# Two transformer blocks on one core: order lists for four engines behind layer 0's self-attention, silu in pairs, MLP products in halves

## The chip, the core and the metric

One core of a Trainium2 chip. The metric is the device time of one execution in microseconds, the median of several runs. Times inside a run come from one profiled execution; they count from the first instruction of its span.

## What is computed

Two blocks in a row on x of 2 batches x 512 tokens x 128 channels, 16 heads of 8 channels.

```python
# layer 0, per batch (c: 128 values, context: 77 x 128, its own layer norm)
x = x + gate_a * (softmax(q k^T / sqrt(8)) v @ W_proj + b_proj)       # 512 x 512 per head, of modulate(ln(x))
x = x + softmax(qc kc^T / sqrt(8)) vc @ W_cproj + b_cproj             # 512 x 77 per head, q of ln(x)
x = x + gate_m * (gelu(modulate(ln(x)) @ W_mlp1 + b) @ W_mlp2 + b)    # 512 hidden
# layer 1, per batch (tokens rolled by 32)
x = x + g_msa * (softmax in windows of 64 tokens @ w_so + b_so)
x = x + g_mca * (softmax over the 16 largest of 77 scores, v, @ w_co + b_co)
x = x + g_mlp * ((silu(a) * b) @ w_m2 + b_m2), a, b = two halves of ln(x) mod @ w_m1    # 2 x 512 hidden
```

## The kernel before

All tensors stay in SBUF; each engine (PE, DVE = VectorE, ACT = ScalarE, POOL, and SP for transfers) runs its own list of instructions in order, and semaphores hold an instruction until its inputs are there. PSUM is cut into six rooms (X0, X1, M0, M1 of one bank, W0, W1 of two); `rooms_in_turns` gives each product its room and its turn in it, `open_room` (L242) makes PE wait until the last user of the room has been read, `read_room` makes the reader wait until it is filled.

Layer 0's self-attention is one loop over 32 heads with a look-ahead (`STEPS`): PE multiplies scores for the maxima (L1504), DVE reduces them (L1221), PE multiplies again with the negated maximum folded in (L1527), ACT takes the exponential (L814), PE multiplies with V (L1542). It ends near 154.6 us.

Behind it stands code in fixed loops, on which this case bears:
- Layer 0's cross-attention, 16 halves (8 heads of 128 tokens each; batch 0 is halves 0 to 7): PE scores (`cross_scores`, L1574), DVE maximum and subtraction (L1275, L1280), ACT exponential (L896), PE turn of the weights (`cross_turn`, L1585), ACT copies (L930), per two halves PE product with V (`cross_pv`, L1597), ACT copy (L832), PE turn (L1557), DVE divide (L1051, L1054). `e` counts the halves; the steps of the next and the last half are written into one turn of the loop on each engine.
- Around it, per batch: turn of the heads (`o_turn`, L1390), projection (`project`, L1401), residual (L1063), layer norm statistics (L973 to L980), its power on POOL (L618), normalization (L985), turn (`ln_T`, L1348), shift and scale on ACT (L767), the next projection.
- The MLP: four chunks of 128 hidden (`mlp_in`, L1673; layer 1 also L1677), gelu (L953) or silu (L958) with the gate product on DVE (`gate_mul`, L1195), and one product `mlp_out` (L1413) over all four chunks that starts when the last chunk is there.
- Layer 1's window attention: per batch eight q and k products (`window_qk`, L1368), their copies on DVE and ACT (L1000, L805), V (L1375, L1009), 8 maxima products with reductions (`window_maxima`, L1612, L1174), the maxima turned, negated (L1178) and sent by SP into rows of Q (L519). Batch 0 is done with its maxima before batch 1 begins, and both before the first window. Then eight windows S (scores, L1641), exponential (L823), V (L1654), turn (L1555), divide (L1185, L1187) in the order of the string `WINDOWS`.
- Layer 1's cross-attention with top-k, 16 halves: PE scores, ACT copy (L902), DVE per half 8 times max (L1294), replace (L1297), max (L1301), replace (L1304); POOL takes the first maximum off (L732), ACT the exponentials of difference (L915) and of what was replaced (`left`, L920), POOL multiplies both (L736), PE turns, and so on as in layer 0. All of the MLP comes behind the last half.

```python
ARRIVE = ({"oT": -1, "out": 1, "lnT": 3, "qc": 5}, {"oT": 2, "out": 3, "lnT": 4, "qc": 5})
WINDOWS = "S0 S1 V0 S2 V1 T0 S3 V2 T1 S4 V3 T2 S5 V4 T3 oT S6 V5 T4 out S7 T5 lnT qc".split()
for e in range(-1, HALVES + 3):        # PE
    if e + 1 < HALVES:
        cross_scores(layer, e + 1)
    if 1 <= e <= HALVES:
        cross_turn(layer, e - 1)
    if e % 2 == 0 and 1 <= e // 2 <= B * NT:
        cross_pv(layer, e // 2 - 1)
```

Of the kernel before, what the change touches and what calls it, by code (L numbers as in the profile page):

```python
# [51 lines left out]
WINDOWS = "S0 S1 V0 S2 V1 T0 S3 V2 T1 S4 V3 T2 S5 V4 T3 oT S6 V5 T4 out S7 T5 lnT qc".split()  # L52
WINDOWS_LATE = {0: ("V6",), 1: ("V7", "T6"), 2: ("T7",)}
# [10 lines left out]
ARRIVE = ({"oT": -1, "out": 1, "lnT": 3, "qc": 5}, {"oT": 2, "out": 3, "lnT": 4, "qc": 5})  # L64
# [28 lines left out]
GATE_SPAN = ((0, 2), (2, 5))  # L93

# [10 lines left out]
def rooms_in_turns():  # L105
# [21 lines left out]
    for layer in range(2):  # L127
        if layer == 1:
            for b in range(B):
                if b:  # L130
                    use("M", "lnT", 3, 1)
                for c in range(NQ):
                    use("M", "qkv", 1, b, "q", c)
                    use("X", "qkv", 1, b, "k", c)
                use("M", "qkv", 1, b, "v")
                for i in range(NT):
                    for half in range(2):
                        use("W", "maxw", b, i, half)
                use("M1", "mT", 1, b)
        if layer == 0:  # L140
            for t in range(STEPS):
                j = t - LOOK - 1
                for q in range(NT):
                    if t < HEADS:
                        use("Y", "max", t, q)
                    for half in first_halves(t - LOOK, q):
                        use("W", "sT", 0, t - LOOK, half)
                    if q == 1 and t % G == 0 and 1 <= t // G <= B * NG:
                        use("Y", "mT", 0, t // G - 1)
                    if q == 2 and j % NT == 0 and 0 <= j < UNITS:  # L150
# [1651 lines left out]
```

## Time and profile before

| | us |
|---|---|
| median of 3 runs | 452.52 (448.51 to 453.73) |
| the profiled execution | 449.5 |
| its span, first to last instruction | 447.7 |

| engine | busy us | share |
|---|---|---|
| PE, products | 362.2 | 81% |
| PE, weight loads (beside products) | 205.6 | 46% |
| DVE | 297.6 | 66% |
| ACT | 203.8 | 46% |
| POOL | 112.0 | 25% |

The engines work side by side, so shares don't add up; what counts in a stretch is which engine's wait ends last. The granted clock is 1.00 when TensorE runs at 2.4 GHz and 0.5 when it runs at 1.2 GHz; between them is a mean over the stretch.

### The profile page before, as it was taken

What the parts mean: (1) busy time and instruction counts of PE and PEld (TensorE: products, weight loads), DVE (VectorE), ACT (ScalarE), POOL (GpSimd) and SP (SyncE); (2) the same over time, 40 slices, a digit from 0 to 9 for tenths busy, and PEclk for the clock granted to TensorE, in tenths of its full rate; (3) what the DMA queues carried; (4) which work ended last, traced back from release to release, by engine and by line L of the source; (5) the groups of instructions that cost most, each with busy time, mean ns of one, the idle gap of its engine ahead of it and who ended that gap; (6) DMA issues with size and microseconds to landing.
All of it is one profiled execution on the core that took longest, in us unless ns stands there. A gap on an engine that the chain in (4) does not pass through costs nothing.

```text
span 447.7 us, 8982 instructions
## 1 busy us (share of the span) xinstructions
PE 362.2 (81%) x3317; PEld 205.6 (46%) x3317; DVE 297.6 (66%) x1279; ACT 203.8 (46%) x303; POOL 112.0 (25%) x130
## 2 busy tenths in 40 slices
PE   2988999999999879898798889956576566674885
PEld 2334223323332357676555467733354334454454
DVE  4677668899893175665437371247989999996342
ACT  2320345666758645667331124413445355654411
POOL 5362110490010120002206000022442544443020
PEclk9995589999999999999999685868876878886999
DMA  7247350410000000000000000000000000000000
GB/s 205 39 152 215 107 159 3 124 46 1 2 1 3 0 1 2 1 2 0 1 1 2 4 3 6 4 1 1 1 1 1 1 2 1 1 1 1 1 24 25
DMA packets 13247, 12.88 MB, mean 29 GB/s; under 512 B 2373, under 2 KB 11681, under 8 KB 13203
## 3 DMA queue, kind: packets, MB, share of 16 engines
q1 hardware_dynamic: 13007, 12.28, 10.1%
q8 instruction: 27, 0.44, 0.4%
q14 instruction: 17, 0.14, 0.1%
q0 software_dynamic: 160, 0.01, 0.0%
q10 hardware_dynamic: 36, 0.01, 0.0%
HBM read 9.41 MB, written 2.63 MB: 27 GB/s over the span
## 4 chain that ended last, share of the span: by engine, by line
PE 53%; DVE 29%; ACT 7%; issue 5%; DMA 3%; POOL 1%; SPq 1%; ACTq 0%; DVEq 0%; POOLq 0%
PE psum L1504 5%; PE psum L1574 5%; PE psum L1542 5%; DVE left L1297 4%; DVE left L1304 4%; PE psum L1527 4%; PE psum L1368 3%; DVE mx L1221 3%; PE psum L1673 3%; DVE top L1294 3%; DVE top L1301 3%; PE psum L1557 3%; PE psum L1585 2%; DVE xhat L985 2%; PE psum L1597 2%
## 5 line engine op out<-in xcount | busy, mean ns | idle before, releaser
L1221 DVE TENSOR_REDUCE mx<-psum 128x1 f32<-128x512 f32 x128 | 81.3, 682 | 17.2 <-PE psum L1504 13.8
L814 ACT ACTIVATE big<-psum 128x1024 f32<-128x1024 f32 x64 | 62.1, 1022 | 42.5 <-PE psum L1527 26.9
L618 POOL TENSOR_TENSOR rstd<-vareps,minus_half 128x4 f32<-128x4 f32 x12 | 12.2, 1020 | 160.0 <-DVE vareps L980 159.8
L1574 PE MATMUL psum<-kblk,qf 128*128 128x308 f32 x128 | 47.2, 501 | 1.1 <-DVE qf L1168 0.8
L1504 PE MATMUL psum<-KS,QS 72*128 72x512 bf16 x112 | 43.8, 420 | 4.9 <-DVE mx L1221 3.7
L1585 PE MATMUL psum<-ident,pr 128*77 128x128 f32 x256 | 38.4, 299 | 10.3 <-POOL pr L736 10.3
L1585 PEld LDWEIGHTS psum<-ident,pr 128*77 128x77 f32 x256 | 34.5, 167 | 18.5 <-POOL pr L736 13.8
L736 POOL TENSOR_TENSOR pr<-pr,early 128x616 f32<-128x616 f32 x16 | 23.9, 1493 | 55.9 <-ACT early L920 34.9
L1542 PE MATMUL psum<-big,V 128*9 128x512 f32 x256 | 34.8, 616 | 0.5 <-ACT big L814 0.5
L1597 PE MATMUL psum<-QS,vc 77*9 77x128 f32 x256 | 13.8, 342 | 24.2 <-ACT QS L930 24.1
L1527 PE MATMUL psum<-QS,KS 75*128 75x512 bf16 x112 | 32.8, 379 | 0.4
L1574 PEld LDWEIGHTS psum<-kblk,qf 128*128 128x128 f32 x128 | 26.9, 231 | 11.5 <-issue 4.9
L1504 PEld LDWEIGHTS psum<-KS,QS 72*128 72x128 bf16 x112 | 10.4, 102 | 46.0 <-issue 21.4
L1051 DVE RECIPROCAL rden<-psum 128x16 f32<-128x16 f32 x24 | 6.0, 250 | 34.8 <-PE psum L1557 34.8
L1297 DVE MATCH_REPLACE8 left<-top,gates 128x77 f32<-128x77 f32 x128 | 26.9, 224 | 0.0
L1304 DVE MATCH_REPLACE8 left<-top,left 128x77 f32<-128x77 f32 x128 | 26.9, 225 | 0.0
L1063 DVE TENSOR_TENSOR x<-psum,x 128x512 f32<-128x512 f32 x12 | 8.3, 690 | 24.6 <-PE psum L1401 14.5
L767 ACT ACTIVATE hT<-psum,mod 128x512 f32<-128x512 f32 x10 | 7.8, 776 | 36.4 <-PE psum L1348 36.4
L930 ACT ACTIVATE big<-psum 77x512 f32<-77x512 f32 x32 | 17.1, 586 | 12.6 <-PE psum L1585 12.5
L1294 DVE MAX8 top<-gates 128x8 f32<-128x77 f32 x128 | 19.4, 225 | 3.8 <-ACT gates L902 3.8
L732 POOL TENSOR_TENSOR early<-gates,top 128x616 f32<-128x616 f32 x16 | 19.6, 1223 | 8.6 <-DVE top L1294 8.2
L902 ACT ACTIVATE gates<-psum 128x616 f32<-128x616 f32 x16 | 10.9, 681 | 22.3 <-PE psum L1574 22.2
(202 smaller groups left out, 666.1 us busy)
## 6 DMA issues: line engine op xcount, KB each, us to landing
QS<-scr_q SPq DMA_DIRECT2D x7, 288.0 KB
KS<-scr_k SPq DMA_DIRECT2D x7, 288.0 KB
scr_q<-qp SPq DMA_DIRECT2D x2, 384.0 KB, 3.1
scr_k<-kp SPq DMA_DIRECT2D x2, 384.0 KB, 3.8
gates<-scr_g SPq DMA_DIRECT2D x2, 320.0 KB, 4.3
early<-in_L_xcond_w_ada_dram SPq DMA_DIRECT2D x1, 576.0 KB, 5.3
scr_k<-kp SPq DMA_DIRECT2D x2, 256.0 KB, 4.3
wmlp<-in_L_xcond_W_mlp_dram SPq DMA_DIRECT2D x2, 256.0 KB, 3.2
```

The source lines that it names most:

```text
L736: pool.tensor_tensor(pr[:, k, :], pr[:, k, :], taken[:, k, :], ALU.mult).then_inc(s_pr, 1)
L814: freed(act.activation(pT[:, u % 2, 1024 * half:1024 * (half + 1)], ps, ACT.Exp), "sT", 0, u, half)
L1221: freed(dve.tensor_reduce(mx[:, n % 3, at:at + 1], ps, AX_X, ALU.max), "max", t, q)
L1294: dve.max(top[:, k, h, 0:8], row(sc, h)).then_inc(s_top, 1)
L1297: dve.match_replace(out=row(left, h), in_to_replace=top[:, k, h, 0:8], in_values=row(sc, h), imm_value=-BIG).then_inc(s_top, 1)
L1304: ins_ = dve.match_replace(out=row(left, h), in_to_replace=top[:, k, h, 8:16], in_values=row(left, h), imm_value=-BIG)
L1504: filled(pe.matmul(ps, QS[b][0:ROWS, h, q * P:(q + 1) * P], KS[b][0:ROWS, h, :], start=True, stop=True), "max", j, q)
L1527: last = pe.matmul(ps[:, t * N:(t + 1) * N], KS[b][0:ROWS + 3, h, kt * P:(kt + 1) * P], QS[b][0:ROWS + 3, h, :], start=True, stop=True)
L1542: last = pe.matmul(ps[QUAD * hh:QUAD * hh + DV, :], V[:, b, kt, G * g + hh, :], pT[:, j % 2, hh * N:(hh + 1) * N], start=(kt == 0), stop=( ...
L1574: last = pe.matmul(ps[:, 512 * a:512 * a + HH // 2 * S], qf[:, b, i * P:(i + 1) * P], kb[:, c0:c0 + HH // 2 * S], start=True, stop=True)
L1585: last = pe.transpose(ps[0:S, t * P:(t + 1) * P], pr[:, e % 2, S * h:S * (h + 1)], ident[:, :])
L1597: last = pe.matmul(ps[q:q + DV, c * P:(c + 1) * P], vc[:, layer, b, h, :], pcT[layer][:, s % 2, h, :], start=True, stop=True)
```

## The change

Everything from the end of layer 0's self-attention on is no longer loops but five tables: `PE_ORDER`, `DVE_ORDER`, `ACT_ORDER` and `POOL_ORDER` list the pieces of each engine one by one, and `RINGS` gives the PSUM rooms of each kind of piece. A piece is `kind.layer or batch.number`: `sc` scores, `T` turn of weights, `C` product with V, `D` its turn and divide, `oT`, `out`, `lnT`, `qc` the steps around it, `mlp0`/`mlp1` the first MLP products, `mo` the halves of `mlp_out`, `wqk`/`wv`/`max`/`mT` the window projections and maxima, `S`/`V`/`W` the window's scores, product and turn with divide, `first8`/`next8` the two parts of a half's top-k, `res`/`stat`/`norm`/`rstd`/`bias` the residual and layer norm.

```diff
+PE_ORDER = pieces("""
+    T.1.9 sc.1.13 oT.3.0 out.4.0 C.1.4 T.1.10 T.1.11 sc.1.14 lnT.5.0 sc.1.15 C.1.5 mlp1.0.0 T.1.12 T.1.13
...
+ACT_ORDER = pieces("""
+    oT.0.1 ex.0 ex.1 T.0.0 T.0.1 ex.2 ex.3 T.0.2 C.0.0 T.0.3 ex.4 lnT.1.1 ex.5 T.0.4 ex.6 T.0.5 ex.7 T.0.6
...
+    copy.14 left.12 mlp.1.0.0 mlp.1.0.1 diff.13 T.1.12 left.13 diff.14 copy.15 C.1.5 T.1.13 left.14
+    mlp.1.0.2 mlp.1.0.3 diff.15 left.15 C.1.6 T.1.14 T.1.15 C.1.7 oT.3.1 lnT.5.1 mlp.1.1.0 mlp.1.1.1
...
+POOL_ORDER = pieces("""
+    bias.2.1 blocks.1.1 rstd.3.1 bias.3.0 rstd.4.0 diff.0 diff.1 mult.0 bias.3.1 mult.1 diff.2 diff.3
+    rstd.4.1 diff.4 mult.2 mult.3 mult.4 diff.5 mult.5 diff.6 mult.6 diff.7 diff.8 mult.7 diff.9 mult.8
...
+RINGS = {('sc', 0): ('W0', 'W1'), ('sc', 1): ('W0', 'W1'), ('T',): ('X1',), ('C',): ('W0',), ('D',): ('X0',),
...
-        pcT = [big[0:S, :, :].rearrange("p k (h t) -> p k h t", h=H),
-               QS[0][0:S, :, :].rearrange("p h t -> p (h t)").bitcast(F32).rearrange("p (k h t) -> p k h t", k=2, h=H)]
+        pW = [[wqr[:, :], kp[:, :, :, :].rearrange("p b j t -> p (b j t)").bitcast(F32)[:, 2 * N:3 * N]],
+              [old[:, B * NT * H * 2 * DV:B * NT * H * 2 * DV + N], wkv[:, :]]]
+        pcT = QS[0][0:S, :, :].rearrange("p h t -> p (h t)").bitcast(F32).rearrange("p (k h t) -> p k h t", k=2, h=H)
...
-            def mlp_out(n, b):
+            def mlp_out(n, b, part):
...
+                for c in (2 * part, 2 * part + 1):
+                    for i in range(NT):
                         last = pe.matmul(ps[:, i * C:(i + 1) * C], gT[:, b, c, i * P:(i + 1) * P],
-                                         gw[n, b][:, c * C:(c + 1) * C], start=(c == 0), stop=(c == NC_ - 1))
-                filled(last, "out", n, b)
+                                         gw[n, b][:, c * C:(c + 1) * C], start=(c == 0 and i == 0), stop=(c == NC_ - 1 and i == NT - 1))
+                if part:
+                    filled(last, "out", n, b)
...
+            def gated_mlp_in(b, pair):
+                for c in (2 * pair, 2 * pair + 1):
+                    ps = open_room(pe, "mlp", 1, b, c)
...
+                ps = open_room(pe, "mlpb", b, pair)
+                for j in range(2):
...
+            for piece in PE_ORDER:
+                kind, args = piece[0], piece[1:]
+                if kind == "sc":
+                    cross_scores(*args)
```

So that pieces may cross, some buffers move: the window exponentials (`pW`) and layer 0's turned weights (`pcT`) leave `big`, in which the gelu and gate outputs lie, and the spread window weights (`wqkF`) leave `left` for `V`; POOL therefore spreads them behind the last product with V of layer 0's self-attention (`spread` in its list). Layer 1's second MLP halves come in pairs of chunks into one room of two banks (`mlpb`).

The new order on two engines. First DVE around layer 1's window maxima, before: L1000 copies q, L985 normalizes batch 1, L1009 adds the bias to V, L1174 reduces maxima, L1178 negates them.

```order
L973 BN_STATS stats<-x 128x6 x4
L977 BN_AGGR mv<-stats 128x2 x4
L980 TENSOR_SCALAR vareps<-mv 128x4
L1000 TENSOR_SCALAR KS<-psum,colsF 128x512 x4
L985 TENSOR_SCALAR xhat<-x,mv,rstd 128x128 x4
L1009 TENSOR_TENSOR QS<-psum,wide 64x64x8 x2
L1174 TENSOR_REDUCE mxw<-psum 128x8 x8
L1178 TENSOR_SCALAR mneg<-psum 64x128
```

The same place now, where the lines are L1057 (q), L1043 (normalization), L1066 (V), L1229 (maxima) and L1235 (negation):

```order
L1057 TENSOR_SCALAR KS<-psum,colsF 128x512
L1229 TENSOR_REDUCE mxw<-psum 128x8 x2
L1057 TENSOR_SCALAR KS<-psum,colsF 128x512
L1229 TENSOR_REDUCE mxw<-psum 128x8
L1066 TENSOR_TENSOR QS<-psum,wide 64x64x8 x2
L1057 TENSOR_SCALAR KS<-psum,colsF 128x512
L1229 TENSOR_REDUCE mxw<-psum 128x8 x2
L1057 TENSOR_SCALAR KS<-psum,colsF 128x512
L1229 TENSOR_REDUCE mxw<-psum 128x8
L1057 TENSOR_SCALAR KS<-psum,colsF 128x512
L1229 TENSOR_REDUCE mxw<-psum 128x8 x3
L1235 TENSOR_SCALAR mneg<-psum 64x128
```

Batch 1's q copies stand between batch 0's reductions, and the negation of batch 0 behind the first reduction of batch 1; before, batch 0's eight reductions and its negation came ahead of all of batch 1. Second, PE at the end of layer 1's top-k, before: L1585 turns weights, L1597 multiplies with V, L1557 turns for the divide, L1673 and L1677 are the first MLP products, L1390 turns the heads, L1401 projects, L1413 is the second MLP product.

```order
L1585 MATMUL psum<-ident,pr 77x128 x8
L1597 MATMUL psum<-QS,vc 9x128 x16
L1557 MATMUL psum<-ident,qp 128x128 x4
L1673 MATMUL psum<-hT,wm 128x512
L1677 MATMUL psum<-hT,wm 128x512
L1673 MATMUL psum<-hT,wm 128x512
L1677 MATMUL psum<-hT,wm 128x512
L1557 MATMUL psum<-ident,qp 128x128 x4
```

And now, with L1627 for the turn of weights, L1639 for the product with V, L1599 for the turn, L1705 and L1709 for the first MLP products, L1428 and L1439 for heads and projection, L1454 for a half of the second MLP product:

```order
L1705 MATMUL psum<-hT,wm 128x512 x2
L1709 MATMUL psum<-hT,wm 128x512 x2
L1454 MATMUL psum<-wm,big 128x128 x8
L1627 MATMUL psum<-ident,pr 77x128 x8
L1599 MATMUL psum<-ident,qp 128x128 x4
L1454 MATMUL psum<-wm,big 128x128 x8
L1627 MATMUL psum<-ident,pr 77x128 x8
L1639 MATMUL psum<-QS,vc 9x128 x16
L1599 MATMUL psum<-ident,qp 128x128 x8
L1428 MATMUL psum<-ident,res 128x128 x4
L1439 MATMUL psum<-gw,res 128x128 x4
```

Batch 0's MLP products all stand ahead of the last turns of batch 1, and nothing stands between these turns, the heads' turn and the projection; before, batch 0's MLP products stood between them.

## Rows read from the trace of the kernel before

**Rows 1.** The page's first line.

```profile
span 447.7 us, 8982 instructions
```

**Rows 2.** Stretches: us, busy PE, PEld, DVE, ACT, POOL, clock, DMA, GB/s.

```profile
154.60:208.40 53.80, 48.48 (x468) 36.04 (x467) 35.78 (x75) 30.57 (x56) 4.68 (x5) 0.97 0.01 2
208.40:232.60 24.20, 20.63 (x152) 14.77 (x151) 7.46 (x32) 11.15 (x17) 4.25 (x4) 1.00 0.00 1
232.60:269.30 36.70, 31.05 (x568) 20.05 (x566) 22.47 (x43) 7.56 (x10) 7.95 (x5) 0.80 0.01 3
269.30:304.90 35.60, 29.72 (x757) 22.63 (x757) 8.67 (x28) 12.97 (x25) 2.28 (x2) 0.64 0.02 4
304.90:407.50 102.60, 64.96 (x533) 44.77 (x531) 99.22 (x807) 50.59 (x85) 44.72 (x34) 0.80 0.00 1
407.50:447.70 40.20, 29.42 (x164) 19.26 (x164) 14.23 (x35) 12.97 (x19) 5.04 (x4) 0.92 0.05 14
```

**Rows 3.** Timeline, layer 0's cross-attention: start us, us, engine line op [idle before <-releaser].

```profile
165.79 1.10 PE L1597 MATMUL psum<-big,vc 77*9 77x128 f32 x16 [2.60 <-ACT big L930]
...
166.82 2.42 PE L1574 MATMUL psum<-kblk,qf 128*128 128x308 f32 x4
...
170.40 1.20 PE L1574 MATMUL psum<-kblk,qf 128*128 128x308 f32 x4
```

**Rows 4.** Timeline, the end of layer 0.

```profile
228.94 3.81 PE L1413 MATMUL psum<-gw,big 128*128 128x128 f32 x32 [0.43 <-ACT big L953]
```

**Rows 5.** Timeline, layer 1's projections and maxima; last row: transfers, us to landing.

```profile
240.54 1.39 DVE L1009 TENSOR_TENSOR QS<-psum,wide 64x512 f32<-64x512 f32 x2
...
247.37 1.29 DVE L1174 TENSOR_REDUCE mxw<-psum 128x8 f32<-128x512 f32 x2 [0.66 <-PE psum L1612]
...
250.92 8.88 PE L1368 MATMUL psum<-hT,left 128*128 128x512 f32 x16 [0.87 <-ACT hT L767]
...
L519 SPq DMA_DIRECT2D KS<-mneg x8: 502/589/592, 249.5 to 271.5; - x8
...
KS<-mneg SPq DMA_DIRECT2D x8, 8.0 KB, 1.9
```

**Rows 6.** Timeline, from the windows to the first top-k.

```profile
286.32 0.42 DVE L1187 TENSOR_TENSOR QS<-psum,rdenw 64x256 f32<-64x256 f32 x1
...
292.21 0.69 DVE L1063 TENSOR_TENSOR x<-psum,x 128x512 f32<-128x512 f32 x1 [5.47 <-PE psum L1401]
...
304.93 1.22 DVE L1294 MAX8 top<-gates 128x8 f32<-128x77 f32 x8 [3.23 <-ACT gates L902]
```

**Rows 7.** Top-k: timeline rows; VectorE's waits (us, times, longest).

```profile
310.50 1.22 DVE L1294 MAX8 top<-gates 128x8 f32<-128x77 f32 x8
...
338.52 1.10 DVE L985 TENSOR_SCALAR xhat<-x,mv,rstd 128x128 f32<-128x128 f32 x4
...
407.99 2.35 DVE L985 TENSOR_SCALAR xhat<-x,mv,rstd 128x128 f32<-128x128 f32 x4
...
DVE top L1294 <- ACT gates L902: 3.8, 3, 3.2
DVE x L1063 <- PE psum L1401: 2.1, 1, 2.1
```

**Rows 8.** Timeline, behind the last match.

```profile
415.14 0.60 ACT L832 ACTIVATE qp<-psum 128x512 f32<-128x512 f32 x1 [1.23 <-PE psum L1597]
...
415.75 1.28 ACT L958 ACT_TABLE_LOAD   x1
...
418.92 0.60 PE L1557 MATMUL psum<-ident,qp 128*128 128x128 f32 x4
...
423.53 0.60 PE L1390 MATMUL psum<-ident,res 128*128 128x128 f32 x4
...
432.18 1.10 PE L1673 MATMUL psum<-hT,wm 128*128 128x512 f32 x2 [0.92 <-issue]
...
444.07 0.69 DVE L1063 TENSOR_TENSOR x<-psum,x 128x512 f32<-128x512 f32 x1 [3.99 <-PE psum L1413]
```

More of the change, by code:

```diff
@@ new lines, in rooms_in_turns @@
+    for t in range(STEPS):
+        j = t - LOOK - 1
+        for q in range(NT):
+            if t < HEADS:
+                use("Y", "max", t, q)
+            for half in first_halves(t - LOOK, q):
+                use("W", "sT", 0, t - LOOK, half)
+            if q == 1 and t % G == 0 and 1 <= t // G <= B * NG:
+                use("Y", "mT", 0, t // G - 1)
+            if q == 2 and j % NT == 0 and 0 <= j < UNITS:
+                use("M0", "pv", 0, j // NT)
+        for item in EARLY.get(t, ()):
+            for kind, key in EARLY_ROOMS[item]:
+                use(kind, *key)
+        if j > 0 and j % NT == 0:
+            use("Y", "pvT", 0, j // NT - 1)
+        for at, key in ((T_OUT, ("oT", 0, 0)), (T_OUT + 2, ("out", 0, 0)),
+                        (T_OUT + 5, ("lnT", 1, 0)), (T_OUT + 7, ("qc", 0, 0))):
+            if t == at:
+                use("Y", *key)
@@ new lines, in turned_weights_out @@
+            def turned_weights_out(layer, f):
+                s = f // 2
+                if s >= 2 and f % 2 == 0:
+                    wait_full(act, "pvc", layer, s - 2)
+                for part in range(2):
+                    ps = read_room(act, "pT", layer, f, part)
+                    h0 = HH * (f % 2) + 4 * part
+                    freed(act.activation(pcT[:, s % 2, h0:h0 + 4, :], ps[0:S, :].rearrange("p (h t) -> p h t", t=P),
+                                         ACT.Copy), "pT", layer, f, part)
@@ new lines, in window_maxima @@
+                ps = row_groups(open_room(pe, "maxw", b, i, half))
+                for c in range(NQ):
+                    for j in range(2):
+                        for w in range(2):
+                            t0, q0 = i * P + w * WIN, QUAD * (2 * half + j)
+                            last = pe.matmul(ps[w * WIN:(w + 1) * WIN, j, c * WIN:(c + 1) * WIN],
+                                             QF[q0:q0 + QUAD, b, c, t0:t0 + WIN], KF[q0:q0 + QUAD, b, c, t0:t0 + WIN],
+                                             start=True, stop=True)
@@ new lines, in window_pv @@
+            def window_pv(u):
+                b, i = steps[u]
+                ps = open_room(pe, "pv", 1, u)
+                if i == 0:
+                    wait_read(pe, "qkv", 1, b, "v")
+                for half in range(2):
+                    wait_read(pe, "sT", 1, u, half)
+                for h in range(H):
+                    c, j = divmod(h, NQ)
+                    p0 = HALF * (j % 2) + WIN * c
+                    last = pe.matmul(ps[QUAD * j:QUAD * j + 2 * DV, c * WIN:(c + 1) * WIN],
+                                     VW[:, b, i, h, :, :].rearrange("p w e -> p (w e)"),
+                                     pW[u % 2][j // 2][:, p0:p0 + WIN], start=True, stop=True)
+                filled(last, "pv", 1, u)
```

1039 lines of the change are left out of this document (471 added, 568 removed), and 23 rows, old and new, of the table RINGS.

## The prediction

> **What bounds the kernel now.** I read the page first: the span is 447.7 us [rows 1], the execution it belongs to took 449.5, and the median of the three runs shown is 452.52, 3.0 above the profiled one. Then I cut the span into seven stretches at the places where the chain of waits changes its engine, and read the busy times of each [rows 2]. The first 154.6 us, layer 0's self-attention, keep their code and their order. After that no engine is full for long. From 154.6 to 208.4 (layer 0's cross-attention) TensorE is busy 48.5 of 53.8 us at a granted clock of 0.97: it is the bound, and only its stalls can go. From 208.4 to 232.6 (the end of layer 0) everything is one chain of small steps. From 232.6 to 269.3 (layer 1's projections and window maxima) TensorE is busy 31.1 and VectorE 22.5 of 36.7, taking turns at a granted 0.80. From 269.3 to 304.9 (windows) VectorE works 8.7 us of 35.6. From 304.9 to 407.5 (top-k) VectorE is busy 99.2 of 102.6: that is its floor. From 407.5 to the end, 40.2 us, it is a chain again. So a new order can win in the second, third, fourth and last of the stretches behind 154.6, and next to nothing in the top-k.
>
> **The change, stretch by stretch.** No matrix product, reduction or exponential is added or dropped; four table loads are added on ScalarE. What follows walks the new lists with the old durations.
>
> *Layer 0's cross-attention.* Now the output product of the heads' weights waits 2.60 us for ScalarE, because the third exponential stands ahead of the copies it needs, and VectorE does a residual and statistics before the third subtraction [rows 3]. Behind that idle time the score products run at half speed, 2.42 us for four where they take 1.20 later [rows 3]: 1.2 more. The new lists put sub.2 ahead of res.0.1, and the copies T.0.0 and T.0.1 ahead of ex.2, so I take both away (3.8) and give 0.5 back for new short waits: the eighth half's scores start about 3.3 earlier than now. From there TensorE has the same work as before.
>
> *The end of layer 0.* Now the out projection of batch 1 stands behind four MLP products, and the last MLP product of 3.81 us starts whole at 228.94 [rows 4]. In the new list one MLP product stands ahead of the last turn and one behind it, so res.1.1 is ready some 5.6 earlier; but lnT.2.1 stands behind mo.2.0.1, and that waits for the fourth gelu, which gives most of it back. The half products let the last MLP product end some 0.9 earlier than it would. Both together: layer 1 starts at 228.4 instead of 232.6, a gain of 4.2.
>
> *Projections and maxima.* Now two batches of projections and two batches of maxima stand one behind the other, 36.7 us. In the new list the windows' scores S.0 may start once the first batch's negated maxima lie in their rows. Of VectorE's 22.5 us in this stretch [rows 2] the list puts one V copy of 1.39, seven of sixteen reductions (two take 1.29, so 4.5) and a negation of about 0.3 behind that point [rows 5], 6.2 in all: 16.3 stay ahead of it. Walking the list I find 5.0 of waits (the first projections, the first maxima, batch 1's transposed activations). Four row transfers of about 0.6 us each to issue and 1.9 to land follow [rows 5], 4.3. Sum 25.6: a gain of 11.1. TensorE's share fits into it: its 31.1 us shrink with the clock, since the second batch's projections, 8.88 of them, ran partly at the lower one [rows 5].
>
> *Windows.* From S.0 to the first eight maxima 35.6 now, of which 17 to the last divide of batch 0 at 286.3, 6 to its residual at 292.2 and 12.7 to the first maximum at 304.93 [rows 6]. The new list has four windows, not six, ahead of that divide, but two maxima products and S.4 ahead of oT.2.0, and S.4 must wait for the second batch's rows, again 4.3 behind a negation. I get 14.8, then 7.4 and 12.7: 34.9, a gain of 0.7.
>
> *Top-k.* A half of 8 heads takes 5.57 us (310.50 less 304.93), sixteen take 89.1 [rows 6, 7]. VectorE's waits inside the stretch are 0.6 for ScalarE's copies (3.8 less the 3.2 ahead of the first) and 2.1 for batch 1's out projection [rows 7]; other VectorE work is then 102.6 - 89.1 - 2.7 = 10.8. The new list moves a normalization (1.1) and two gate products (taken at a residual's 0.69 each) in and two divides (an estimate of 0.5 each) out: +1.5 [rows 6, 7]. Two normalizations now stand beside a POOL product each. Now one such takes 2.35 us where another takes 1.10 [rows 7], so I add 2.5. Walking ScalarE's list with its silu pairs I find each score copy ready 1.5 us or more before VectorE asks, so no wait is added, and the old 2.7 go: 89.1 + 10.8 + 1.5 + 2.5 = 103.9, a loss of 1.3. That cover is thin: a silu pair costs ScalarE two loads of 1.28 and two silus, about 4 us, where it has some 2 us idle per half, twice.
>
> The Trainium skill, ScalarE: Activation LUTs, section What ACT_TABLE_LOAD costs, says that each switch costs the load of 1283 ns and a drain of some 1380 ns, and that calls should be batched by table set, against what this change does. The trace agrees with the load and shows no drain: the copy before it ends at 415.74 and the load begins at 415.75 [rows 8]. By the row four more loads are 5.1 us of ScalarE, by the rule 10.6, of which two would lie on the last chain, 2.8 more than I count.
>
> *The tail.* Now, behind the last match at 407.5, the last turn stands behind four MLP products (418.92), and the turn for the out projection behind four more (423.53); the second batch's MLP starts at 432.18 and the last residual at 444.07 [rows 8]. In the new list the gates gate.0.2 and gate.0.3 follow the last match, mo.5.0.1 holds T.1.15 back until +5.0, and the turn oT.3.1 comes at +9.2 instead of +16.0: 6.8 gained. From there to the MLP is as before. Its two half products let the first half run ahead of the last two gates: 10.7 instead of 11.9 to the last residual. The exp load ahead of the last left.15 costs 0.5, counted in the +9.2. Sum: a gain of 8.0.
>
> Sum: 4.2 + 11.1 + 0.7 - 1.3 + 8.0 = 22.7. On the profiled 449.5 that is 426.8. The median of the runs shown is 3.0 above that execution; I add about half of this and forecast 428.
>
> **Bounds.** The walk is optimistic, since every list is in order and a late input stops all that stands behind it. Unshown is TensorE's clock under the new order. It is granted 0.80 in the maxima and 0.64 in the windows now [rows 2]; I took mixed clock for the first and the low one for the second. As estimates from the 29.7 and 31.1 us of TensorE there [rows 2]: at full clock in the windows too a quarter of the 29.7 goes, 8 us (420); at the low one in the maxima too 0.3 of the 31.1 come back, 9 us (437).
>
> **Rivals.**
> *A cold TensorE in layer 1* (437). For it: maxima of 64 columns with waits between them are where the clock falls now [rows 2]. Against: they stand among dense projections now.
> *Top-k waits* (436). POOL's list puts diff.3, rstd.4.1 and diff.4 ahead of mult.2, so turned weights come late; if half of the sixteen halves wait 1 us each, +8. For it: VectorE's floor has no room. Against: the only score copy that hangs on mult.2 is some 3 us early.
> *The stalls only move* (449.5): in-order lists stop at pieces that come late, as S.4 ahead of oT.2.0 does, and eat the gain. For it: four engines' lists cross in hundreds of places. Against: the tail's 6.8 and the maxima's overlap rest on few steps.
> *Slower: layer 0's cross-attention at half clock* (455 and up). It is the one long stretch where TensorE is the bound, at 0.97 [rows 2], and there half speed costs its whole time: four score products take 2.42 instead of 1.20 [rows 3]. If finer order leaves more pauses and it runs low, 48.5 us of busy time become up to 97; above about half of the stretch the 24 us gained are gone. Against: the lists take waits out there. The Trainium skill, TensorE: Matmul & The Clock Gate, section HAM oscillation, says that pauses between bursts throw the array back to half clock again and again; the drop at 166.8 behind an idle wait agrees.
>
> **How the numbers follow.** Forecast (420 to 433) 0.50, cold TensorE 0.18, top-k waits 0.17, stalls moved 0.09, slower 0.06. The range of 418 to 443 holds the first three. About 1% (448 to 457) is what a measurement tells from no change: faster is 0.85, the same 0.09, slower 0.06.
>
> **What would show it.** Right: layer 1's first projection near 228, the first window scores near 254, the first top-k maximum near 289, the last match near 392, 32 us behind it. Wrong: a top-k of more than 106 us (the second rival), windows later than 260 (the first), granted clock under 0.9 in layer 0's cross-attention (the last), or a tail still above 37 us.

## The result and the profile after

The changed kernel takes 435.53 us (median of 4 runs, 431.75 to 440.47) where the kernel before takes 452.97 beside it: a ratio of 0.9606, 95% interval 0.9539 to 0.9674. Forecast were 428 and 418 to 443. In a second comparison it took 434.34, ratio 0.9644 (0.9593 to 0.9695). Ratios, here and below, are of the runs within 1.5% of the fastest of their kernel, medians of all runs. The profiled execution took 431.75, 17.7 us below that of before; the sum had promised 22.7 on the same base.

The page's first line of the changed kernel:

```profile
span 430.0 us, 9048 instructions
```

Its stretches, cut where those of [rows 2] were cut (first cross scores, last turn of layer 0's weights, first projection of layer 1, first window scores, first top-k maximum, last match, end); columns as there:

```profile
152.80:201.40 48.60, 45.97 (x469) 35.99 (x466) 38.43 (x75) 31.12 (x56) 9.17 (x10) 1.00 0.01 2
201.40:227.70 26.30, 20.79 (x149) 14.32 (x150) 12.22 (x32) 11.41 (x17) 7.55 (x5) 1.00 0.00 1
227.70:256.20 28.50, 27.21 (x487) 16.70 (x489) 19.18 (x38) 7.45 (x10) 2.26 (x2) 0.96 0.02 4
256.20:291.50 35.30, 29.40 (x845) 23.31 (x839) 11.96 (x34) 13.11 (x25) 1.02 (x1) 0.69 0.02 4
291.50:395.20 103.70, 71.19 (x545) 48.23 (x546) 103.32 (x812) 57.88 (x93) 48.38 (x37) 0.80 0.00 1
395.20:430.00 34.80, 23.90 (x155) 16.59 (x154) 10.78 (x31) 10.14 (x16) 3.79 (x3) 0.85 0.06 16
```

Measured from the first row of one operation to the first row of the next (the last match: to its end), in the profiles of both kernels:

| stretch | before | after | moved | predicted |
|---|---|---|---|---|
| start to first cross scores | 154.7 | 152.9 | -1.9 | 0 |
| to layer 1's first projection | 77.9 | 74.8 | -3.0 | -4.2 |
| to the first window scores | 36.7 | 28.6 | -8.2 | -11.1 |
| to the first top-k maximum | 35.6 | 35.3 | -0.4 | -0.7 |
| to the last match | 102.6 | 103.7 | +1.1 | +1.3 |
| to the end | 40.1 | 34.8 | -5.3 | -8.0 |

The first line is no gain of the change. In thirteen profiles of kernels whose lists agree up to there, the first cross scores come between 151.4 and 158.8 us. So what follows compares stretches, not the clock time of an event. Three stretches gave less than promised: 1.2, 2.9 and 2.7 us.

What is new at the end of layer 0, in the timeline of VectorE (DVE), POOL and TensorE (PE):

```profile
195.03 4.07 DVE L1043 TENSOR_SCALAR xhat<-x,mv,rstd 128x128 f32<-128x128 f32 x4
212.20 2.88 DVE L1043 TENSOR_SCALAR xhat<-x,mv,rstd 128x128 f32<-128x128 f32 x4 [1.13 <-POOL rstd L686]
219.46 4.02 DVE L1043 TENSOR_SCALAR xhat<-x,mv,rstd 128x128 f32<-128x128 f32 x4 [1.12 <-POOL rstd L686]
...
195.27 1.28 POOL L749 TENSOR_TENSOR x<-x,gb 128x512 f32<-128x512 f32 x1
196.50 2.26 POOL L757 TENSOR_TENSOR kblk<-kcT,mask 128x1232 f32<-128x1232 f32 x1
212.12 2.10 POOL L706 COPY QS<-blank 128x2304 f32<-128x2304 f32 x1
219.39 1.27 POOL L749 TENSOR_TENSOR x<-x,gb 128x512 f32<-128x512 f32 x1
220.62 2.27 POOL L757 TENSOR_TENSOR kblk<-kcT,mask 128x1232 f32<-128x1232 f32 x1
...
201.44 1.10 PE L1627 MATMUL psum<-ident,pr 128*77 128x128 f32 x8 [1.57 <-ACT pr L943]
```

The same kernel's view of the normalization's line from 194.9 to 224 us (shortest, median and longest instruction in ns; first and last start):

```profile
L1043 DVE TENSOR_SCALAR xhat<-x,mv,rstd x12: 334/352/2305, 195.0 to 223.1; 128x128 f32<-128x128 f32 x12
```

Four instructions of some 0.34 us each make a normalization; undisturbed it takes 1.1, as in [rows 7]. Here three take 4.07, 2.88 and 4.02 us, and one single instruction 2305 ns, which is as long as the POOL instruction beside it (2.26, 2.27). Behind the first of them TensorE waits 1.57 us for the last exponential.

The windows, the top-k's table load and the tail, in the timeline of the same kernel:

```profile
274.99 1.64 PE L1667 MATMUL psum<-KS 32*64 32x64 f32 x64 [1.25 <-DMA KS<-mneg]
...
377.92 0.80 ACT L966 ACTIVATE early<-left,negbig 128x616 f32<-128x616 f32 x1
378.73 1.28 ACT L990 ACT_TABLE_LOAD   x1
...
404.18 0.63 PE L1428 MATMUL psum<-ident,res 128*128 128x128 f32 x4 [0.77 <-DVE res L1111]
413.31 3.75 PE L1705 MATMUL psum<-hT,wm 128*128 128x512 f32 x4 [0.92 <-issue]
...
426.42 0.69 DVE L1120 TENSOR_TENSOR x<-psum,x 128x512 f32<-128x512 f32 x1 [2.21 <-PE psum L1454]
```

The top-k's waits of VectorE (us, times, longest):

```profile
DVE top L1328 <- ACT gates L951: 1.4, 1, 1.4
```

Stretches around TensorE's last pause, columns as above:

```profile
407.00:411.00 4.00, 0.00 (x0) 0.00 (x0) 2.76 (x14) 0.00 (x0) 1.02 (x1) 0.59 0.01 2
411.00:414.00 3.00, 1.77 (x5) 1.21 (x6) 0.16 (x1) 1.55 (x2) 1.27 (x1) 0.50 0.00 0
```

S.4 waits for the second batch's rows, as feared. The turn oT.3.1 comes 9.0 us behind the last match (395.2), as walked. But TensorE then pauses 4.6 us for the normalization, its granted clock falls to 0.50, the lower of its two levels (1.2 GHz), and the first two gated products (two rows of matmul each, x4) take 3.75 us; before, the first of them took 1.10 [rows 8].

### The profile page after: what moved, and what is told of

The parts are those of the page before. It is cut to its first block, busy times and chain, and to the rows that moved or that the text cites. A ratio compares the mean times of both kernels' runs of the same rounds, so it can differ in the third digit from the quotient of the medians.

```text
span 430.0 us, 9048 instructions
## 1 busy us (share of the span) xinstructions
PE 354.7 (82%) x3317; PEld 203.0 (47%) x3317; DVE 305.6 (71%) x1279; ACT 209.1 (49%) x307; POOL 111.8 (26%) x130
## 3 DMA queue, kind: packets, MB, share of 16 engines
q1 hardware_dynamic: 13007, 12.28, 10.7%
## 4 chain that ended last, share of the span: by engine, by line
PE 50%; DVE 30%; issue 8%; ACT 4%; DMA 3%; POOL 3%; SPq 1%; ACTq 0%; POOLq 0%
PE psum L1546 6%; PE psum L1584 5%; DVE left L1331 5%; DVE left L1343 5%; PE psum L1616 4%; PE psum L1569 4%; PE psum L1627 4%; DVE top L1328 4%; PE psum L1404 3%; DVE mx L1267 3%; DVE top L1340 3%; DVE xhat L1043 3%; PE psum L1454 3%; PE psum L1652 2%; PE psum L1667 2%
## 5 line engine op out<-in xcount | busy, mean ns | idle before, releaser
L1627 PE MATMUL psum<-ident,pr 128*77 128x128 f32 x256 | 39.0, 300 | 20.1 <-POOL pr L794 18.2
L1616 PE MATMUL psum<-kblk,qf 128*128 128x308 f32 x128 | 44.8, 482 | 7.0 <-DVE qf L1225 4.5
L977 ACT ACTIVATE QS<-psum 77x512 f32<-77x512 f32 x64 | 34.9, 588 | 30.8 <-PE psum L1627 30.5
L1627 PEld LDWEIGHTS psum<-ident,pr 128*77 128x77 f32 x256 | 32.2, 162 | 28.0 <-POOL pr L794 21.7
L1616 PEld LDWEIGHTS psum<-kblk,qf 128*128 128x128 f32 x128 | 24.6, 213 | 18.2 <-DVE qf L1225 6.3
L1043 DVE TENSOR_SCALAR xhat<-x,mv,rstd 128x128 f32<-128x128 f32 x48 | 24.6, 573 | 5.0 <-POOL rstd L686 5.0
L1229 DVE TENSOR_REDUCE mxw<-psum 128x8 f32<-128x512 f32 x16 | 10.9, 690 | 12.7 <-PE psum L1652 12.5
```

The lines of the kernel that those rows point to most:

```text
L977: freed(act.activation(pcT[:, s % 2, h0:h0 + 4, :], ps[0:S, :].rearrange("p (h t) -> p h t", t=P), ACT.Copy), "pT", layer, f, part)
L1043: last = dve.tensor_scalar(xhat[:, b, i, :], x[:, b, i, :], mv[:, b, i, 0:1], rstd[:, b, i:i + 1], ALU.subtract, ALU.mult)
L1616: last = pe.matmul(ps[:, 512 * a:512 * a + HH // 2 * S], qf[:, b, i * P:(i + 1) * P], kb[:, c0:c0 + HH // 2 * S], start=True, stop=True)
L1627: last = pe.transpose(ps[0:S, t * P:(t + 1) * P], pr[:, e % 2, S * h:S * (h + 1)], ident[:, :])
```

## The experiments

Theory: the missing 5 us are POOL pieces that block VectorE's normalizations at the end of layer 0, TensorE's return at half clock in the tail, and TensorE as the bound of the interleaved projections. Rivals: these are cover and something else sets the end; S.4's wait for rows; the table loads. Each kernel was timed in five rounds against the kernel before. "The changed kernel" is the base unless another is named. Line numbers in rows can be off by up to three, since lines were added or wrapped.

| run | median us | ratio to before (95%) |
|---|---|---|
| c0_after | 434.34 | 0.9644 (0.9593 to 0.9695) |
| e1_pool_early | 429.31 | 0.9533 (0.9487 to 0.9580) |
| e2_warm_tail | 436.46 | 0.9662 (0.9607 to 0.9716) |
| e3_s4_later | 434.54 | 0.9645 (0.9591 to 0.9698) |
| e4_pool_topk | 433.75 | 0.9627 (0.9581 to 0.9674) |
| e5_warm_short | 432.77 | 0.9597 (0.9561 to 0.9633) |
| e6_silu_last | 442.35 | 0.9811 (0.9774 to 0.9848) |
| e7_proj_apart | 441.57 | 0.9793 (0.9748 to 0.9838) |
| e8_all | 423.94 | 0.9369 (0.9303 to 0.9436) |
| e9_whole | 437.35 | 0.9703 (0.9640 to 0.9766) |
| e10_batch0_first | 431.22 | 0.9593 (0.9543 to 0.9642) |
| e11_front | 430.31 | 0.9533 (0.9476 to 0.9590) |

**The changed kernel again.** No edit.

> The changed kernel once more, on the chip and in the rounds of the next three, so that each of them has a time to stand against. Expected 0.96 of the kernel before, as in its first comparison (0.9606), 435 us by a median of 453. Every theory expects the same here: normalizations of 2.9 to 4.1 us at the end of layer 0, a granted clock near 0.5 around the first gated MLP product of the tail.

Time as expected. Its profile shows something that the first one did not: from the first cross scores to layer 1's first projection it needs 77.7 us, not 74.8. The stretches around the end of the cross-attention (columns as above):

```profile
200.00:205.00 5.00, 3.79 (x42) 2.73 (x43) 0.86 (x3) 3.37 (x6) 0.27 (x1) 0.67 0.00 0
205.00:210.00 5.00, 4.23 (x16) 2.37 (x14) 1.10 (x4) 0.62 (x2) 0.00 (x0) 0.65 0.00 0
```

Behind TensorE's wait for the last exponential the granted clock falls to about two thirds over ten us. Of nine profiles with POOL's list unchanged up to there, six show this fall and need 77.5 us or more for the stretch; the other three need 74.8, 74.8 and 76.4. The 76.4 (the run with S.4 later) has a fall of its own further on: 0.50 from 225.6 to 229.0, behind TensorE's wait of 2.23 us for the third long normalization, and the last MLP product there takes 5.34 us instead of 3.74.

**POOL's pieces early.**

```diff
-rstd.1.0 rstd.1.1 bias.1.0 rstd.2.0 spread bias.1.1 blocks.1.0 bias.2.0 rstd.2.1 blanks
-rstd.3.0 bias.2.1 blocks.1.1 rstd.3.1 bias.3.0 rstd.4.0 diff.0 diff.1 mult.0 bias.3.1
+rstd.1.0 bias.1.0 rstd.1.1 bias.1.1 spread blanks rstd.2.0 bias.2.0 rstd.2.1 bias.2.1
+rstd.3.0 bias.3.0 rstd.3.1 bias.3.1 blocks.1.0 blocks.1.1 rstd.4.0 diff.0 diff.1 mult.0
```

> POOL's list alone is changed: spread and blanks stand behind the second normalization's bias (POOL is idle there for 29 us), every bias behind its own normalization, the two layer 1 blocks behind the last normalization of layer 0. Theory (POOL's copies and products block the normalization that starts beside them): the three normalizations of 4.07, 2.88 and 4.02 us go back to 1.1 each; the last two lie on the chain, so layer 1's first projection comes 4.7 us earlier and the whole ends 4 to 6 us earlier (430, 0.950 of before). Rival (the chain there is set by gelu and the MLP products, the normalizations are cover): the normalizations shrink, the projection starts within 1 us of now, time within 1 us of the changed kernel.

The three normalizations in this run, what stands beside POOL's copy now, the last turn, and POOL's two products with a query copy beside them:

```profile
195.42 1.10 DVE L1042 TENSOR_SCALAR xhat<-x,mv,rstd 128x128 f32<-128x128 f32 x4
210.44 1.12 DVE L1042 TENSOR_SCALAR xhat<-x,mv,rstd 128x128 f32<-128x128 f32 x4 [1.13 <-POOL rstd L685]
217.71 1.11 DVE L1042 TENSOR_SCALAR xhat<-x,mv,rstd 128x128 f32<-128x128 f32 x4 [1.13 <-POOL rstd L685]
...
166.58 2.11 POOL L705 COPY QS<-blank 128x2304 f32<-128x2304 f32 x1
...
166.34 0.80 DVE L1314 TENSOR_TENSOR gates<-psum,cmax 128x616 f32<-128x616 f32 x1
167.64 0.80 DVE L1309 TENSOR_REDUCE cmax<-psum 128x8 f32<-128x616 f32 x1 [0.50 <-PE psum L1615]
...
199.68 1.10 PE L1626 MATMUL psum<-ident,pr 128*77 128x128 f32 x8
...
231.13 4.48 POOL L756 TENSOR_TENSOR kblk<-kcT,mask 128x1232 f32<-128x1232 f32 x2
233.91 0.75 DVE L1056 TENSOR_SCALAR KS<-psum,colsF 128x512 f32<-128x512 f32 x1 [0.34 <-PE psum L1403]
```

All three are back at 1.1, TensorE's wait ahead of the last turn is gone, the granted clock stays at 1.00 there (in all four profiles of kernels with this list), the stretch takes 70.2 us instead of 74.8 or 77.7, and the end comes 5.0 us earlier. The theory holds; the rival (cover) falls. What POOL stands beside matters: its copy of 2.11 us beside a subtraction and a reduction that read PSUM leaves them at 0.80, and a query copy that reads PSUM beside its products stays at 0.75.

**Unread products in TensorE's pause**, nine and then five, ahead of the wait in the last `ln_T`.

```diff
 ps = open_room(pe, "lnT", n, b)
+if (n, b) == (5, 1):
+    for i in range(9):    # five in the second run
+        pe.matmul(ps, W["wm1"][:, 0:P], hT[:, 0, :], start=True, stop=True)
 pe.wait_ge(s_hat[b], n + 1)
```

> Nine products of 128x512 whose result nobody reads (the turn behind them overwrites it) fill TensorE's pause of 4.6 us ahead of the last turned normalization. Theory (the tail was 2.6 us longer than predicted because TensorE paused there and came back at half clock): granted clock 1.0 behind the pause, the first eight gated products take 4.1 us instead of 6.0, the turn 0.63 instead of 1.08, the end comes 2 to 2.5 us earlier (433). Rival (the gates wait for ScalarE's table load and silu, not for the products): products faster, end unchanged within 0.5 us. A second rival: the added products keep TensorE busy past the moment when the normalization is there, and the end comes later.

> As the run with nine unread products ahead of the last turned normalization, with five: nine took 7.9 us at full clock, 0.87 each and not 0.5, and held the turn back 3.1 us; five take 4.4 us, less than the pause of 4.6. Theory (cold TensorE lengthens the tail): no delay of the turn, first eight gated products 3.8 us instead of 6.0, last match to last residual 28.7 us instead of 31.1, the end 2 to 2.5 us earlier. Rival (silu and its table load set the pace): last match to last residual above 30.5.

The nine added products, and then the five with the first gated ones behind them:

```profile
410.64 7.89 PE L1386 MATMUL psum<-hT,wm 128*128 128x512 f32 x18
```

```profile
412.23 4.46 PE L1384 MATMUL psum<-hT,wm 128*128 128x512 f32 x10
418.52 1.96 PE L1706 MATMUL psum<-hT,wm 128*128 128x512 f32 x4 [0.92 <-issue]
```

Nine took 7.89 us and held the turn back: the second rival of that run, and a mis-sizing of mine (each product is two rows of matmul, 0.87 us and not 0.5; the eight products of the expectations are eight such rows). The gated products still ran at full clock, 1.96 us for the first two instead of 3.75. Five fit, and the last match is followed by the last residual after 28.5 us instead of 31.1: the clock was the 2.6 us. The time shows it weakly, 0.9597 against 0.9644, with intervals that overlap.

**S.4 behind the out turn.**

```diff
-S.4 oT.2.0 S.5 out.3.0      # PE; on ACT: S.4 oT.2.0
+oT.2.0 S.4 out.3.0 S.5      # on ACT: oT.2.0 S.4
```

> On TensorE and ScalarE the fifth window's scores S.4 stand behind the out turn oT.2.0, and S.5 behind out.3.0. Theory (S.4's wait for the second batch's rows, which land at 274.95, holds the turn back): the turn starts at 274.6 instead of 276.57 and out.3.0 at about 276.3 instead of 279.2, so the first top-k maximum comes 2 to 3 us earlier and the end as much (433). Rival (what bounds the stretch is TensorE at half clock, which does the same products in either order; the last windows now come later and delay the second batch): within 1 us of the changed kernel.

The stretch from the first window scores to the first maximum took 33.2 us (35.3 and 34.6 in the two profiles of the changed kernel); the time did not move. With the old order and nine unread products that stretch took 32.7 in one profile, with five 37.0, and both are alike up to there; a gain of 2 us can't be told from that. Inconclusive.

**POOL's order in the top-k.**

```diff
-diff.2 diff.3 rstd.4.1 diff.4 mult.2 mult.3 ... bias.4.0 diff.11 mult.11 rstd.5.0 diff.12 bias.4.1 bias.5.0
+diff.2 mult.2 diff.3 diff.4 rstd.4.1 mult.3 ... bias.4.0 bias.4.1 mult.6 ... diff.11 mult.11 rstd.5.0 diff.12 bias.5.0
```

> POOL's list in the top-k alone: mult.2 ahead of diff.3, diff.4 ahead of rstd.4.1, and both biases of the fifth normalization in an earlier pause. Theory (a normalization waits for the POOL instruction beside it, and VectorE has no slack here): the two normalizations of 3.1 and 1.9 us go back to 1.1 each, the top-k takes 101.0 us instead of 103.7, the end comes 2 to 3 us earlier (432). Rival (VectorE's gain is given back as a wait for a later score copy or POOL's product): normalizations shorter, top-k still above 103.

The two normalizations of the top-k in this run's timeline:

```profile
327.33 1.11 DVE L1042 TENSOR_SCALAR xhat<-x,mv,rstd 128x128 f32<-128x128 f32 x4
...
375.16 1.10 DVE L1042 TENSOR_SCALAR xhat<-x,mv,rstd 128x128 f32<-128x128 f32 x4
```

These are the fourth and fifth layer norms' normalizations, 1.1 us each where the changed kernel needs 3.08 and about 1.9; the top-k goes from 103.7 to 102.1. The four profiles with this order have 101.2 to 102.1, the nine of the changed kernel and its variants without it 103.5 to 104.8. In time that is 0.9627 against 0.9644, not resolved alone.

**The silu pairs undone.**

```diff
-left.12 mlp.1.0.0 mlp.1.0.1 ... left.14 mlp.1.0.2 mlp.1.0.3 diff.15 left.15 C.1.6 T.1.14 T.1.15 C.1.7
+left.12 ... left.14 diff.15 left.15 C.1.6 T.1.14 mlp.1.0.0 mlp.1.0.1 T.1.15 C.1.7 mlp.1.0.2 mlp.1.0.3
```

The gated products and the gates stand behind the last match too.

> Undoes the silu pairs: batch 0's gated products, silus and gates stand behind the last exponential again, the first pair ahead of the last turn, the MLP products behind the last turn. Theory (the pairs took the MLP of batch 0 off the end): from the last match to the last residual 36 us or more instead of 31.1, top-k 1.5 us shorter (two gates and no loads in it), end 3 to 5 us later (438 to 440). Rival (the top-k pays for it: ScalarE's loads, 5.1 us, and the gates on VectorE cost as much as the tail gains): within 1.5 us of the changed kernel.

Last match to last residual 39.5 us instead of 31.1, the top-k 103.5 instead of 103.7, the end 7.5 us later (0.9811 against 0.9644, of 450): the pairs are worth more than the 3 to 5 expected, and the top-k pays nothing for them. The turn for the out projection:

```profile
413.24 0.60 PE L1428 MATMUL psum<-ident,res 128*128 128x128 f32 x4
```

It comes 16.7 us behind the last match (396.5), where the pairs have it at 9.0 and the kernel before had it at 16.0 [rows 8]: nearly all of the tail's gain is this one step.

**Projections and maxima apart again.**

```diff
-wqk.0.3 lnT.3.1 max.0.0.0 max.0.0.1 wqk.1.0 ... max.1.2.1 S.0 S.1 V.0 S.2 V.1 max.1.3.0
+wqk.0.3 wv.0 max.0.0.0 ... max.0.3.1 mT.0 lnT.3.1 wqk.1.0 ... wqk.1.3 wv.1 max.1.0.0 ... max.1.3.1 mT.1 S.0
```

> Undoes the interleaving of layer 1's projections and maxima: batch 0's projections, its maxima, batch 1's projections, its maxima, then the windows, on TensorE and VectorE; all other lists as changed. Theory (the overlap is the largest gain, 8.1 us from first projection to first window scores): that stretch goes from 28.7 to 36 us or more, of which some 2 us come back because S.4 no longer waits for rows, the end 5 to 7 us later (440 to 442). Rival (the windows are bound by the half clock and the top-k's start hangs on something else): the end less than 3 us later.

This run's stretches from first projection to first window scores, and from there to the first maximum:

```profile
231.30:273.20 41.90, 34.67 (x569) 21.69 (x568) 22.87 (x43) 7.56 (x10) 2.26 (x2) 0.77 0.01 3
273.20:300.70 27.50, 24.10 (x755) 18.95 (x754) 8.51 (x28) 12.98 (x25) 1.02 (x1) 0.79 0.02 5
```

The first stretch takes 41.9 instead of 28.6 us, at a granted clock of 0.77 instead of 0.96; the windows (27.5) give 7 to 8 of the 13 back, with no maxima and no wait for rows among them. The end is 6.7 us later by the ratios, as expected: beside the silu pairs the overlap is the largest part of the gain. The run does not bring the old stretches back (36.7 and 35.6), since all other lists stay changed: the two together take 69.4 us here, 63.8 in the changed kernel and 72.3 before, so some 3 us of the gain in them have another source, which no run separates.

**MLP products whole again.** Each waits for all four chunks, its halves stand together behind the fourth.

```diff
-mlp1.0.1 mo.5.0.0 T.1.14 D.1.5 mo.5.0.1 T.1.15
+mlp1.0.1 T.1.14 D.1.5 mo.5.0.0 mo.5.0.1 T.1.15
```

> Undoes the MLP products in two pieces: each starts when all four chunks are there, and its two halves stand one behind the other. Theory (the second batch's half runs ahead of the last two gates): the last product starts at about +1.6 us, as the first half starts now 1.6 us before the last gate ends; batch 0's whole product waits for the last gates and delays the last turn; layer 0 loses up to 1 us. End 1.5 to 4 us later (436 to 438). Rival (the pieces only shift work inside pauses): within 1 us.

The last turn of the weights and the last MLP product in this run's timeline:

```profile
401.51 1.04 PE L1627 MATMUL psum<-ident,pr 128*77 128x128 f32 x8
425.71 3.81 PE L1454 MATMUL psum<-gw,big 128*128 128x128 f32 x32 [1.59 <-DVE big L1252]
```

The last product waits 1.59 us for the last gate, the last turn comes 5.6 behind the last match instead of 4.6; together the 2.5 us by which this tail is longer (33.65 against 31.1). The end is 2.7 us later by the ratios. Layer 0's stretch, 78.7, is the longest of the six with the lowered clock (the others 77.5 to 78.1), but in this profile the clock falls a second time, to 0.50 from 224.4 to 227.8, and the last MLP product takes 4.94 us instead of 3.74. That is more than the difference, so the 1 us expected there does not show.

**The four edits together**: early POOL pieces, S.4 later, top-k order, five unread products.

> The four edits that the earlier runs spoke for, together: POOL's pieces early, S.4 behind the out turn, POOL's top-k order, five unread products ahead of the last turned normalization. Theory (they act in different stretches and add up): cross-attention to first projection 70.3 us, first window scores to first top-k maximum 33, top-k 102, last match to last residual 28.5; end at 423, 0.94 of the kernel before. Rival (an earlier start of one stretch is given back by the next, as part of POOL's gain was in the projections): 427 to 430.

Of this run's stretches, layer 0 from the first cross scores on (both parts in one row), the top-k and the tail:

```profile
157.30:227.60 70.30, 66.49 (x618) 50.36 (x616) 42.61 (x107) 42.40 (x72) 12.36 (x13) 1.00 0.01 1
...
291.40:392.90 101.50, 71.30 (x545) 49.57 (x546) 100.84 (x812) 57.96 (x93) 47.21 (x36) 0.80 0.01 1
392.90:424.90 32.00, 25.41 (x165) 17.06 (x163) 10.79 (x31) 10.08 (x16) 3.77 (x3) 1.00 0.06 17
```

423.94 us, 10.4 below the changed kernel's 434.34 (12.4 by the ratios) and 6.3% below the kernel before by the ratio, 5.8% by the medians. Stretch by stretch the gains add up: the 70.3 is there, the top-k takes 101.5, the tail runs at a granted 1.00. The windows (34.8) show no gain from S.4. Of this run's profiled 426.72, 157.3 are self-attention, near the upper end of its scatter.

**Batch 0 first**, on top of the four edits.

VectorE's list follows in the same order; TensorE's, in part:

```diff
-wqk.1.1 max.0.2.0 wqk.1.2 max.0.2.1 max.0.3.0 wqk.1.3 max.0.3.1 max.1.0.0 mT.0 ... wv.1 max.1.2.1 S.0 S.1 V.0 S.2 V.1
+wqk.1.1 max.0.2.0 max.0.2.1 max.0.3.0 max.0.3.1 wqk.1.2 mT.0 wqk.1.3 max.1.0.0 max.1.0.1 max.1.1.0 S.0 S.1 V.0 S.2 V.1 max.1.1.1 wv.1
```

> On top of the four edits: on TensorE and VectorE batch 1's last key and query projections, its V projection and its later maxima stand behind batch 0's negated maxima or among its windows. Theory (TensorE, busy 27 of 28.3 us, bounds the interleaved stretch, so batch 1's products ahead of the first window scores are on the path): first projection to first window scores 25 to 26 us instead of 30, the end 2 to 4 us before that of the four edits. Rival (VectorE's reductions or the row transfers bound it): stretch above 28.5, end the same. A second rival: the pushed products come back in the windows, where the clock is low, and S.4 waits longer for its rows: stretch shorter, windows longer by as much.

This run's stretches, from first projection to first window scores, to S.4, to the first maximum:

```profile
225.00:250.70 25.70, 23.23 (x399) 13.48 (x398) 17.09 (x35) 7.45 (x10) 6.72 (x4) 1.00 0.01 4
250.70:282.40 31.70, 25.53 (x594) 20.48 (x585) 9.94 (x21) 6.80 (x13) 0.00 (x0) 0.54 0.02 4
282.40:296.00 13.60, 12.16 (x338) 9.66 (x338) 4.28 (x17) 6.39 (x12) 1.02 (x1) 0.70 0.01 2
```

S.4 and the turn of batch 0's normalization in its timeline:

```profile
282.44 1.64 PE L1668 MATMUL psum<-KS 32*64 32x64 f32 x64 [1.25 <-DMA KS<-mneg]
290.25 0.81 PE L1387 MATMUL psum<-ident,xhat 128*128 128x128 f32 x4
```

First projection to first window scores takes 25.7 us, 3.3 less: batch 1's pieces were on the path, and VectorE's as much as TensorE's. Added up row by row to the end of batch 0's negation, VectorE works 15.0 us instead of the 16.4 of the four edits alone, and stands idle 5.9 instead of 7.3. But the second rival took it back and more: the pushed maxima run at a granted 0.54, batch 1's rows come 31.7 us behind the first scores, S.4 waits for them, and the turn of batch 0's normalization, which stands behind S.6, begins at 290.25, 4.6 us after that normalization ended. 45.3 us of windows instead of 34.8; the end 7.3 us later.

**The old start of the cross-attention**, on top of the four edits.

```diff
-sub.1 sub.2 res.0.1 stat.1.1 sub.3 norm.1.1     # VectorE
+sub.1 res.0.1 stat.1.1 sub.2 norm.1.1 sub.3
-T.0.0 T.0.1 ex.2                                # ScalarE
+T.0.0 ex.2 T.0.1
-sc.0.4 C.0.0                                    # TensorE
+C.0.0 sc.0.4
```

> On top of the four edits (424 us, 70.2 us from the first cross scores of layer 0 to layer 1's first projection in three profiles alike) the start of layer 0's cross-attention in its old order: the first heads' product ahead of the fifth half's scores, the third exponential ahead of the second turned copies, residual and statistics ahead of the third subtraction. Theory (the prediction's 3.3: a wait of 2.6 and 1.2 at half speed, less 0.5): TensorE waits some 2.6 us near 12 us into the stretch, its clock falls for the next scores, the stretch takes 73 to 74 us and the end comes 3 to 4 us later (427 to 428). Rival (TensorE's later pauses in that stretch absorb it, the pause there is cover): the wait is there, the stretch stays below 71.5, the end within 1.5 us of the four edits.

The first heads' product and the scores behind it, in this run's timeline:

```profile
169.86 1.10 PE L1640 MATMUL psum<-QS,vc 77*9 77x128 f32 x16 [2.61 <-ACT QS L977]
170.90 2.42 PE L1617 MATMUL psum<-kblk,qf 128*128 128x308 f32 x4
```

The wait of [rows 3] is back (2.61, there 2.60), and with it the 2.42 us of scores at half clock. The stretch takes 74.9 instead of 70.2, 4.6 more. The ratio is 0.0164 higher, 7.4 us, with an uncertainty of some 4 us in that difference, so the stretch may be all of it.

## Why the prediction was right, and where it was not

The sign and the range hold, the parts that carry the gain are the ones named, and the stretches moved in the predicted order of size. In the profile the sum was 5 us too large: three steps missed by 6.8, and the 1.9 by which the self-attention happened to be shorter hides part of it. The median missed by 7.5, because the profiled execution is the fastest of the four. 435.5 lies above the 420 to 433 to which I gave 0.50, and near the 436 and 437 of two rivals that did not happen as written; that the range holds it is in part luck.

Undone one at a time, the silu pairs cost 7.5 us, the overlap of projections and maxima 6.7, the start of the cross-attention 4.6 (by its stretch, on top of the four edits) and the halves of the MLP products 2.7. That is 21.5, where the change gained some 16 by the second comparison; as an estimate, the difference is about what POOL's pieces took back (4.6 and more, below).

*Layer 0.* "I take both away (3.8)" is right and even small: undoing it alone costs 4.6 (the overview had not counted this stretch among those that can win). The end of layer 0 had more in it than the 0.9 I left it: without POOL's pieces the whole is 70.2 against 77.9, a gain of 7.6 where I had 4.2. The step that failed is one that is not in the working: POOL's list was walked in the top-k only, where I priced two normalizations beside POOL at 2.5 by the 2.35 and 1.10 of [rows 7]. The same list puts spread, blocks.1.0, blanks and blocks.1.1 right behind the rstd that three normalizations of layer 0 wait for. The price stood in my own rows; it was not asked for at the other places. It cost 4.6 us, and 1.6 to 3.9 more where the clock fell, so 1.2 were missing in the first profile and about 4 in most others.

*Projections and maxima.* "TensorE's share fits into it" failed. I walked VectorE's list (16.3 of work, 5.0 of waits) and found 25.6. Added up row by row to the end of batch 0's negation, the work is right (16.4), but VectorE stands idle 7.5, and its waits there are for TensorE's products. The largest of them (us, times, longest; the other two are 2.1 for the projections and 1.3 for V):

```profile
DVE mxw L1229 <- PE psum L1652: 3.7, 5, 1.7
```

TensorE has 27.2 us of products in the 28.5 that the stretch took, at a granted 0.96: it is the bound. That batch 1's pieces were in the way the run with batch 0 first shows (25.7); pushed out in its order, they cost more than they gave.

*Windows.* -0.4 against -0.7, but the eight profiles with this part of the lists as in the changed kernel have 32.7 to 37.0, so the agreement is luck. S.4 waits for rows as walked; whether that costs the end anything stayed open.

*Top-k.* +1.1 against +1.3, and no wait for a score copy inside it (the one of 1.4 us stands ahead of the first maximum), so the second rival (436 by waits) did not happen, though the time came out near its number. The two normalizations took 3.08 and about 1.9 where I had 2.35 each. The table loads cost their 1.28 and no drain: `left.12` ends at 378.72 and the load begins at 378.73. The Trainium skill, ScalarE: Activation LUTs, section What ACT_TABLE_LOAD costs, has a drain in its price; this trace shows none, as before.

*The tail.* oT.3.1 at +9.0 (walked: +9.2). "From there to the MLP is as before" and "10.7 to the last residual" failed by the clock: 13.1 from the first gated product to the last residual. Before, TensorE had batch 0's second MLP product to do in that pause, and stood idle 1.07 of it; the change took that work away, and with it the clock. Five unread products bring the 2.6 back. In the timeline of the kernel before:

```profile
425.83 3.74 PE L1413 MATMUL psum<-wm,big 128*128 128x128 f32 x32
430.64 0.63 PE L1348 MATMUL psum<-ident,xhat 128*128 128x128 f32 x4 [1.07 <-DVE xhat L985]
```

*Rivals.* A cold TensorE in layer 1 did not come where I put it (0.96 in the projections, 0.80 before) but in the tail, where I had not looked. Layer 0's cross-attention ran at 1.00, and in six of nine profiles its last ten us at about two thirds: the slow rival's place, at 3 us and not at 24.

## What to carry to other kernels

When a list moves work on POOL, ask what VectorE does beside each moved piece, at every place and not only where VectorE is the bound: here a normalization from SBUF to SBUF waited out the whole POOL instruction (up to 2.3 us), work that reads PSUM did not. When a change takes work away ahead of a pause of TensorE, price the products behind the pause at the lower clock; a few unread products that fit into the pause kept it here (4.46 us of them in a pause of 4.6). And when two lists are interleaved, sum the busy time of every engine over the new stretch before trusting a walk of one.

## What the hardware showed that I had not expected

One normalization instruction of 128x128 took up to 2305 ns instead of some 340 beside a POOL product, while reductions (0.80), subtractions (0.80) and query copies (0.75), all of which read PSUM, kept their time beside POOL's copy of 2.11 us and its two products of 4.48 together. The Trainium skill, SBUF — State Buffer, section Who interferes with whom, says that VectorE and GpSimd share one pair of ports under an exclusive lock, that `tensor_scalar` can take it, and that whoever issues first has it for the whole instruction while the other is blocked. The trace agrees where POOL came first: ten of the changed kernel's normalization instructions are slowed, and each ends 0.08 us behind the end of a POOL instruction. The other order, VectorE first, was not looked at.

The clock's fall at the end of the cross-attention is not the same from run to run: with the same lists up to there six of nine profiles show it and three don't, some 3 us apart, two of the nine show another fall further on, and the profile read first was one of the two without either. One profile alone would have put the whole loss down to the normalizations.
